# A hand-written order for the first three batches of an adaptive-norm state-space block on one core

## The reference, cut to what matters

```python
sa, ca, ga, sb, cb, gb = split(silu(c) @ wmod)          # per batch, 256 channels each; ga, gb kept away from 0
h = layernorm(x) * (1 + ca) + sa
u, gate = split(h @ W_in.T)                              # 256 and 256 channels
b, dt = u @ W_state.T, min(softplus(u @ W_dt.T + b_dt), 10)   # 128 states each
decay = exp(-dt * (softplus(A_log) + 1e-4))
state[t] = decay[t] * state[t-1] + (1 - decay[t]) * b[t]      # over the 512 tokens
x1 = x + ga * ((state @ W_C.T * silu(gate) + h * D) @ W_out.T)
h = layernorm(x1) * (1 + cb) + sb;  h_prev = h one token earlier
xk, xr = mix of h and h_prev by mu_k, by mu_r
out = x1 + gb * (sigmoid(xr @ W_r.T) * (relu(xk @ W_k.T)**2 @ W_v.T))
```

## Time and profile before

| what | value |
|---|---|
| median of 3 runs | 375.15 us |
| profiled execution | 375.2 us, its span 373.4 us |
| PE, DVE, ACT, POOL busy | 96%, 81%, 82%, 69% of the span |
| first matmul of step 3 (batch 0's K) | 47.80 us |
| first matmul of steps 4 and 5 | 68.39 and 89.63 us |
| last matmul starts, last DVE instruction ends | 367.2, 370.9 us |

### The profile page before, as it was taken

The page is one execution under the profiler, slowest core; times in us unless marked ns, Lnnn a source line. Parts: engine busy times, 40 slices in busy tenths (PEclk is TensorE's granted clock), DMA queues, the critical chain, the costliest instruction groups (busy, mean ns, idle before and its releaser), DMA issues.

```text
span 373.4 us, 5613 instructions
## 1 busy us (share of the span) xinstructions
PE 359.3 (96%) x1702; PEld 275.8 (74%) x1705; DVE 303.2 (81%) x640; ACT 307.7 (82%) x416; POOL 259.3 (69%) x269
## 2 busy tenths in 40 slices
PE   7999799999999999999999999999999999999784
PEld 4776477777778777777778777777877777776563
DVE  2788967988979798988979898888979788877654
ACT  4466779899898989989898989989898989977372
POOL 2072658969686887969686986968687894855560
PEclk9999999999999999999999999999999999999999
DMA  8931111130313132040313122040303021010111
GB/s 280 395 109 56 56 59 56 58 114 0 117 53 112 59 108 61 32 139 2 113 57 114 56 73 97 2 141 29 114 0 114 1 76 38 21 38 0 56 55 60
DMA packets 18607, 29.16 MB, mean 78 GB/s; under 512 B 1168, under 2 KB 9616, under 8 KB 18448
## 3 DMA queue, kind: packets, MB, share of 16 engines
q1 hardware_dynamic: 18144, 28.71, 22.6%
q10 hardware_dynamic: 432, 0.09, 0.1%
HBM read 20.40 MB, written 8.39 MB: 77 GB/s over the span
## 4 chain that ended last, share of the span: by engine, by line
POOL 46%; issue 39%; PE 7%; DVE 4%; ACT 2%; DMA 1%; POOLq 1%; SPq 0%; DVEq 0%; ACTq 0%
POOL xr_lo L773 10%; POOL xk_lo L773 7%; POOL z_lo L830 6%; POOL h_lo L773 6%; POOL k_lo L773 6%; POOL state_lo L820 4%; POOL rstd L783 3%; PE slot L224 3%; DMA w_in<-weights_in 1%; PE slot L238 1%; PE slot L352 1%; DVE stats L566 1%; POOL prev L814 1%; POOL spread L781 1%; POOL spread L780 1%
## 5 line engine op out<-in xcount | busy, mean ns | idle before, releaser
L809 POOL TENSOR_TENSOR rstd<-mv,half_neg 128x4 f32<-128x4 f32 x16 | 16.1, 1007 | 54.0 <-DVE mv L579 54.0
L452 ACT ACTIVATE prev<-slot,mod,mix_prev 128x512 f32<-128x512 f32 x64 | 46.3, 787 | 5.8 <-PE slot L231 5.8
L773 POOL TENSOR_TENSOR xk_lo<-xk,xk_hi 128x512 fp32r<-128x512 f32 x32 | 40.9, 1298 | 9.8 <-ACT xk_hi L463 9.0
L224 PE MATMUL slot<-h_hi,wf_hi 128*128 128x512 f32 x128 | 45.9, 399 | 0.4 <-ACT h_hi L478 0.4
L224 PE MATMUL slot<-h_hi,wf_lo 128*128 128x512 f32 x128 | 45.6, 397 | 0.0
L773 POOL TENSOR_TENSOR xr_lo<-xr,xr_hi 128x512 fp32r<-128x512 f32 x32 | 42.5, 1330 | 0.0
L830 POOL TENSOR_TENSOR z_lo<-z,z_hi 128x512 fp32r<-128x512 f32 x26 | 33.7, 1295 | 10.9 <-ACT z_hi L459 7.4
L773 POOL TENSOR_TENSOR k_lo<-k_act,k_hi 128x512 fp32r<-128x512 f32 x30 | 38.2, 1293 | 3.8 <-ACT k_act L533 3.8
L773 POOL TENSOR_TENSOR h_lo<-h,h_hi 128x512 fp32r<-128x512 f32 x30 | 38.4, 1303 | 3.1 <-ACT h_hi L478 3.1
L231 PE MATMUL slot<-ident,xn 128*128 128x128 f32 x256 | 35.9, 274 | 2.8 <-DVE xn L603 2.1
L231 PEld LDWEIGHTS slot<-ident,xn 128*128 128x128 f32 x256 | 29.7, 141 | 11.3 <-issue 4.7
(11 more groups left out here) (123 smaller groups left out, 1002.5 us busy)
## 6 DMA issues: line engine op xcount, KB each, us to landing
x_tok<-x_tok_in SPq DMA_DIRECT2D x16, 512.0 KB, 3.6
x_ch<-x_ch_in SPq DMA_DIRECT2D x16, 512.0 KB, 3.7
x_out<-wmod SPq DMA_DIRECT2D x15, 512.0 KB, 3.0
wmod<-wmod_in SPq DMA_DIRECT2D x1, 1024.0 KB, 10.1
w_in<-weights_in SPq DMA_DIRECT2D x1, 1024.0 KB, 11.5
w_in<-weights_in SPq DMA_DIRECT2D x1, 768.0 KB, 5.6
wmod<-wmod_in SPq DMA_DIRECT2D x1, 512.0 KB, 6.6
x_out<-wmod SPq DMA_DIRECT2D x2, 256.0 KB, 2.0
```

Of the source, the lines that this page charges most:

```text
L224: ins = nc.tensor.matmul(out, w[:, c, at + d * P:at + (d + 1) * P], x[:, c, :], start=first, stop=last)
L452: return nc.scalar.activation(prev[:, mix, i, 1:T + 1], ps_n[:, i, :], ACT.Identity, bias=mod_at(SHIFT2 + i, k), scale=mix_prev[:, mix, i, ...
L773: nc.gpsimd.tensor_tensor(lo, x, hi.bitcast(F32), ALU.subtract).then_inc(done, 1)
L809: nc.gpsimd.tensor_tensor(rstd2[:, c % 2], mv2[:, c % 2, 1, :], half_neg[:], ALU.pow).then_inc(rstd2_ok, 1)
```

## The change

The steps 0 to 2 are written out by hand and the loop starts at step 3. The order in each engine's list is new for these three batches. Loads: the early weights come in two transfers, first the 512 columns for L256 (512 KB), and the gate's 256 columns (256 KB) behind the first part of `wmod`; the rest of `wmod` now comes ahead of the third batch of tokens. Batch 0's front is not split: its `dt`, `b` and `g` are plain float32 products of `w_front`, `w_early` and `h`; with it `h_hi` and `h_lo` of batch 0 are gone. The front of batch 2 is emitted ahead of step 3. In PSUM, V and the `x1` transposes move to slot 3, K, the `xn2` transposes and (from batch 3 on) `g` to slot 2; `g` of batches 0 to 2 stays in slot 3 and the `x1` transposes of batch 0 in slot 2; the transposes of batches 1 and 2 for `h` go to slot 1. The `keep_warm` matmuls go from 13 + 11 + 5 + 6 to 10 + 4. In the loop one thing changes on PE: R's low piece of half 0 goes ahead of all of `y`. On ACT the halves of `h` are made in the order 0, 1 (before: 1, 0). `low_h(2)` stands on POOL, `h_lo` of batch 1 on DVE.

```diff
-        STEPS = range(0, NB + 4)
+        STEPS = range(3, NB + 4)
+        def ps_h(k):
+            return slot[1] if 0 < k <= WHOLE else slot[0]
+        def ps_gate(k):
+            return slot[3] if k <= WHOLE else slot[2]
+        def ps_x1(k):
+            return (slot[2] if k == 0 else slot[3])[:].rearrange(...)
...
 # SP
-            sp.dma_start(w_in[:, 0:CH * 3 * C], w_d[:, 0:CH * 3 * C]).then_inc(s_w, 16)
+            sp.dma_start(w_early[:, :, 0:GATE], w_early_d[:, :, 0:GATE]).then_inc(s_w, 16)
             sp.dma_start(wmod[:, :, 0:2 * C], wmod_cols[:, :, 0:2 * C]).then_inc(s_wmod, 16)
+            sp.dma_start(w_early[:, :, GATE:], w_early_d[:, :, GATE:]).then_inc(s_wgate, 16)
...
 # PE
-            keep_warm(slot[0][:, 0, :], 13)
+            keep_warm(slot[0][:, 0, :], 10)
...
+            first_norm(0)
+            keep_warm(slot[3][:, 0, :], 4)
+            pe.wait_ge(front_ok, 1)
+            pe.wait_ge(h0_ok, 1)
+            half(dt_out, w_front, 0, h[:, 0], 0, first=True)
+            pe.wait_ge(h_ok, 1)
+            half(dt_out, w_front, 0, h[:, 0], 1, last=True).then_inc(dt_ps, 1)
+            half(b_out, w_front, NS, h[:, 0], 0, first=True)
+            half(b_out, w_front, NS, h[:, 0], 1, last=True).then_inc(b_ps, 1)
+            pe.wait_ge(s_wgate, 16)
+            half(g_out, w_early, GATE, h[:, 0], 0, first=True)
+            half(g_out, w_early, GATE, h[:, 0], 1, last=True).then_inc(g_ps, 1)
+            modulation(4, 3, slot[2][:, 1, :])
+            state_out(0)
+            first_norm(1)
+            modulation(7, 5, slot[2][:, 1, 3 * NB:]).then_inc(mod_ps, 1)
+            attention_out(0, 0)
+            front_high(1)                 # dt and b, 8 matmuls; waits wsplit_lo, hhi_ok, z_ok[1]
+            front_low(1)                  # 4 matmuls
+            attention_out(0, 1)
+            gate_high(1); gate_low(1)     # 8 and 4 matmuls
+            first_norm(2)                 # waits x1_ok of batch 0
+            token_stats(0)                # the x1 transposes
+            state_out(1)
+            gate_high(2)                  # waits hhi_ok 2, silu_ok 2
+            front_high(2)                 # waits z_ok of batch 1
+            to_channels(ps_n, xn2).then_inc(t3_ps, 1)   # waits xn2a_ok, xn2b_ok
+            front_low(2); gate_low(2)     # wait hlo_ok
+            attention_out(1, 0); attention_out(1, 1)
...
 # PE, in the loop
+                if live(d):
+                    pe.wait_ge(xrlo_ok[0], d + 1)
+                    half(r_out, wl_hi, MIX_R, xr_lo, 0)
                 if live(b):
                     # y, high part (or state_out)
...
-                if live(d):
-                    pe.wait_ge(xrlo_ok[0], d + 1)
-                    half(r_out, wl_hi, MIX_R, xr_lo, 0)
...
 # ACT, ahead of the loop, in this order
+            ln1_apply(0); modulated(0, 0) -> h0_ok; modulated(0, 1) -> h_ok
+            exponential(0); decays(0); table load; ln1_apply(1); gate_silu(0)
+            wl_hi for K, R; modulated(1, 0..1); rounded_h(1); ln1_apply(2)
+            table load; exponential(1); decays(1); table load
+            wl_hi for V, OUT; wy_hi; gate_silu(1); modulated(2, 0..1); rounded_h(2)
+            table load; ln1_apply(3); previous x2 of batch 0; exponential(2)
+            previous x2; rounded_xk(0, 0); decays(2); rounded_xk(0, 1); table load; gate_silu(2)
 # DVE, ahead of the loop, behind the splitting of the early weights
+            ln1_stats(1); clipped(0); ln1_mean_variance(1); driven(0); scanned(0)
+            ln1_apply(1); ln1_stats(2); ln1_mean_variance(2); gated(0); ln1_apply(2)
+            h_lo of batch 1; rest_of_modulation(); clipped(1); ln1_stats(3); after_attention(0)
+            driven(1); scanned(1); ln1_mean_variance(3); after_transpose(0); gated(1)
+            normalised(0); ln1_stats(4); ln1_mean_variance(4); ln1_apply(3)
+            mixing(0, 0); clipped(2); mixing(0, 1); after_attention(1)
+            driven(2); scanned(2); after_transpose(1)
 # POOL, ahead of the loop
+            ln1_scale(0); ln1_scale(1); low part of K; ln1_scale(2); low parts of R, V
+            second_scale(0); ln1_scale(3); low_h(2); low parts of OUT and wy
```

More of the change, by code:

```diff
@@ new lines, in state_out, with attention_out @@
+            def state_out(k):
+                pe.wait_ge(state_ok, k + 1)
+                for i in range(CH):
+                    last = nc.tensor.matmul(ps_y[:, i, :], w_y[:, i * P:(i + 1) * P], state[:], start=True, stop=True)
+                last.then_inc(y_ps, 1)
+            def attention_out(k, i):
+                pe.wait_ge(h_ok, k + 2)
+                pe.wait_ge(z_ok[i], k + 1)
+                last = half(o_out, w_late, OUT, z, i, first=(i == 0), last=(i == CH - 1))
+                if i == CH - 1:
+                    last.then_inc(o_ps, 1)
@@ L449, in gate, with ln1_apply @@
                 nc.scalar.activation(r_gate[:], ps_r[:], ACT.Tanh, scale=0.5).then_inc(tanh_ok, 1)
+            def ln1_apply(k):
+                act.wait_ge(shift1_ok, k + 1)
+                before(act, t1_ps, k)
+                for t in range(TT // 2):
+                    last = nc.scalar.activation(xn1[:, t, :], x_tok[:, k % 3, t, :], ACT.Identity,
+                                                bias=shift1[:, k % 2, t:t + 1], scale=rstd1[:, k % 2, t:t + 1])
+                last.then_inc(xn1a_ok, 1)
             def previous(mix, i, k):
@@ new lines, in gate_silu @@
+            def gate_silu(k):
+                act.wait_ge(g_ps, k + 1)
+                before(act, yg_ok, k)
+                nc.scalar.activation(silu[:], ps_gate(k)[:], ACT.Silu).then_inc(silu_ok, 1)
+            ln1_apply(0)
+            act.wait_ge(mod1_ok, 1)
+            act.wait_ge(t1_ps, 1)
+            modulated(0, 0).then_inc(h0_ok, 1)
+            modulated(0, 1).then_inc(h_ok, 1)
+            exponential(0)
+            decays(0)
+            nc.scalar.preload_act_table_set("silu_and_others")
@@ L639, in _, with mixing @@
+            def mixing(k, i):
+                if i == 0:
+                    dve.wait_ge(first_ok, k + 1)
+                dve.wait_ge(prev_ok[i], k + 1)
+                for x, mix, done, low in ((xk, KEY, xk_ok, xklo_ok), (xr, REC, xr_ok, xrlo_ok))[::1 if i == 0 or k == LAST else -1]:
+                    before(dve, low[i], k)
+                    mixed(x, mix, i, k, done[i])
             nc.vector.memset(half_neg[:], -0.5).then_inc(consts_ok, 1)
@@ new lines, in _ @@
+            ln1_mean_variance(2)
+            gated(0)
+            ln1_apply(2)
+            for i in range(CH):
+                dve.wait_ge(hhi_ok, 1)
+                nc.vector.tensor_tensor(h_lo[:, i], h[:, 1, i], h_hi[:, i].bitcast(F32), ALU.subtract).then_inc(hlo_ok[i], 1)
+            rest_of_modulation()
+            clipped(1)
+            ln1_stats(3)
+            after_attention(0)
+            driven(1)
+            scanned(1)
+            ln1_mean_variance(3)
+            after_transpose(0)
@@ L669, in _ @@
+            gated(1)
+            normalised(0)
+            ln1_stats(4)
+            ln1_mean_variance(4)
+            ln1_apply(3)
+            mixing(0, 0)
+            clipped(2)
+            mixing(0, 1)
+            after_attention(1)
+            driven(2)
+            scanned(2)
+            after_transpose(1)
             for s in STEPS:
                 a, b, c, d = s, s - 1, s - 2, s - 3
+                if live(b) and b > WHOLE:
+                    scanned(b)
+                if live(c):
+                    normalised(c)
```

460 lines of the change are left out of this document (263 added, 197 removed).

## The result

The changed kernel takes 373.42 us, the median of seven runs (372.59 to 374.37), against 375.15 for the kernel before in the same series. It is 1.7 us faster in the median, where 3.3 were forecast. The ratio of the two sets of runs, which is not quite the quotient of the medians (0.9954), is 0.9943, with an interval of 0.9928 to 0.9958, so about 2.1 us. The profiled executions stand further apart, 375.2 and 372.59; the latter is the fastest of its seven. So the traces show 2.6 us, and 0.9 of the forecast's error lies between the runs and not in that trace.

The account below looks back on a forecast made before the run. PE, busy in 96% of the span, was taken as the bound; -2.3, +1.2, -2.4 and +0.1 up to step 4 made -3.3, loop and tail 0: 375.2 to 371.9 us, own range 370.5 to 373.3, stated range 370.0 to 374.1.

Parts of the forecast that it names:

- the walk: New engine order followed with trace prices to step 4's first matmul: 65.05 against 68.39; then loop and tail.
- Step A: Opening: less weight load ahead and only half 0 of h needed start batch 0's front at 11.95, not 14.24: -2.3 us.
- Step B: Batch 0's front on PE: 8 whole matmuls, 6.85 us, instead of 24 split ones, 5.6: +1.2 us.
- Step C: Opening behind 14.24: eleven zero matmuls gone, -2.4 us if the waits they stood in don't come back.
- D: Waits in the new order up to step 4: 3.05 us in sum against 2.95 before, +0.1; could be off by -1.5 to +2.
- one sign of being wrong: Opening: a PE wait over 1.5 us was listed among what would show the forecast wrong.
- rival 2: Opening's waits are longer: DVE's after_transpose pass comes once more into PE's path, 2.1 us, giving 374.0; chance 14%.
- Step E: Loop, 13 split steps: R's low piece ahead of y moves the wait to state_lo; 0, bounds -2.2 to +2.3 us.
- rival 1: Loop: state_lo is early enough, so R's piece ahead of y gains 0.17 us a step, giving 369.7; chance 8%.
- rival 4: Loop: the wait moved from state_hi to state_lo costs more, +2.3 us, giving 374.2; chance 3%.
- Step F: Tail: y of the last batch comes 0.47 later, but DVE's later wait absorbs it; 0, at worst +0.47 us.
- The clock: Opening: with 10 zeros PE runs at 1.2 GHz from 6.2 until batch 0's front, +4.4 us, giving 376.3; chance 5%.

Follow-up runs that it names:

- run 3: Changed kernel with R's low piece back behind y's high part in every step; 373.03 us, ratio to the kernel before 0.9942.
- run 5: Changed kernel with the early input weights in one transfer of 768 KB again; 373.94 us, ratio to the kernel before 0.9949.
- run 6: Changed kernel with batch 0's front split again and eleven zero matmuls instead of four; 374.58 us, ratio to the kernel before 0.9968.
- run 7: Changed kernel with batch 1's h transposes in slot 0 again; 381.15 us, ratio to the kernel before 1.0152.
- run 1: The changed kernel again, no edit; 373.26 us, 372.57 to 375.76 in ten runs, ratio to the kernel before 0.9952.
- run 9: Changed kernel with 8 and 5 zero matmuls in two PE waits of the tail; 372.95 us, ratio to the kernel before 0.9931.
- run 8: The kernel before with batch 0's front as whole products and nothing else of the change; 376.09 us, ratio to the kernel before 1.0003.
- run 4: Changed kernel with batch 2's state_hi ahead of the relu of K(0) in step 3; 372.31 us, ratio to the kernel before 0.9932.
- run 2: Changed kernel with 13 instead of 10 zero matmuls in front; 373.30 us, ratio to the kernel before 0.9942.
- run 10: Changed kernel with 12 instead of 10 zero matmuls in front and 2 ahead of the first modulation; 374.02 us, ratio to the kernel before 0.9955.
- run 11: Changed kernel with early state_hi of batch 2, zeros in the tail's waits and more zeros in the opening; 372.34 us, ratio to the kernel before 0.9916.
- run 12: The kernel before with 8 and 5 zero matmuls in the tail's waits; 374.94 us, ratio to the kernel before 0.9984.

## Why the prediction was right, and where its size was off

- **Which way, and where.** Right: the time is won between the start and step 4 (2.32 us in the traces), the loop gives 0.28 us, where the forecast had 0, and the tail nothing. The order of the waits in the opening and three of their sizes are as walked. The size was not: the median, 373.42, is 0.12 above the forecast's own range of 370.5 to 373.3 and lies in the stated one, to 374.1, only by the room that was left for the rivals, not by the walk; the gain is about half of what was forecast. Runs 3, 5, 6 and 7 each take one part of the change back; the new order on DVE and POOL, the zeros left out and batch 2's front ahead of step 3 were not tested singly, and what they give is read from the walk and the traces.
- **Step A** was 0.2 us too large in the trace (front at 12.12, not 11.95), 0.6 in run 1's. The term that failed is the landing of the first modulation's weights, which the walk took to be over when the weight product ends; from there to the modulation 0.2 us pass in the changed kernel's trace (8.22) and 0.7 in run 1's (8.60). In run 9's there is no such wait (7.88), and the front starts at 11.70, before the walk's time. The walk's other bound, `xn1` until 9.85, wasn't the last: it is ready at 9.84 and at 9.52 in these traces, and the transposes follow the modulation (10.03, 10.41). Part of the gain hangs on when loads land.
- **Step B** was right: the whole front took 6.95 us (12.12 to 19.07), 6.85 forecast. Run 6 shows that in the new order the unsplit front wins 0.6 to 0.9 us; run 8 that alone it wins nothing.
- **Step C** with **D**: step 3's first matmul was 0.13 late against the walk. Up to step 4 another 0.9 is lost. 0.67 of it is the wait for `xn2(1)`, 1.52 instead of 0.85: the walk had the wait but not that a DVE instruction stands still for POOL's subtraction (run 4 gets 0.64 back by one edit). The other 0.2 is spread over gaps, the largest 0.3 us ahead of the `h` transposes at 62.37. By the letter one sign of being wrong came up, a wait over 1.5 us on PE in the opening. It is rival 2 in kind, in a third of its size (0.67 of 2.1) and at another wait, `xn2(1)` and not `z(1)`.
- **Step E** was right in mechanism and size: 0.02 us a step between before and after, 0.00 between run 3 and the changed kernel. Rivals 1 and 4 are out.
- **Step F** was right: 50.51 us on both sides.
- **The clock** was weighed as one case, 5% for a loss large enough to turn the sign, and not as a loss in part of the runs. It was that: in the opening 1.6 us in run 3's profiled execution and about 1.7 in run 7's. In the changed kernel's own trace the rise came later than the walk had it: all ten zeros ran at the lower level and ended at 5.75, not 5.4. Of the seventeen runs of the changed kernel three are over 374.2 (374.37, 374.72, 375.76), but in the first two the span is 371.5 and 371.9, and 2.8 to 2.9 us lie outside it, 1 us more than in most runs; only the third, with a span of 373.6 and a clock of 0.990, looks like run 3's (373.4, 0.990). What came ahead of such a loss was ten zeros, of which at most three at the higher level, and waits of 0.4 to 0.9 us on one side or both of L334. That the fewer zeros are its cause isn't shown: in the 21 runs with more of them (2, 10 and 11) the longest span is 1.6 us over the shortest of its kernel, but run 9 has no such loss in six either.
- **The account.** By the traces: forecast -3.3; the wait for `xn2(1)` +0.7, the front's start +0.2, the loop -0.3, the rest +0.1 make -2.6. This pair of traces flatters the change: the span after, 370.8, is among the shortest, that before, 373.4, the longest of the ten runs beside run 1 with a granted clock of 0.996 or more (372.9 to 373.4). The changed kernel's four such runs there have 370.7 to 371.1, so 2.2 us less in the middle. With the tail filled on both sides it is 2.0 us (runs 9 and 12). All of these lie within the interval of the comparison, 1.6 to 2.7 us, as the median's 1.7 does. How much the landing of the load and how much the clock take of the difference to the trace is open, since most of the runs have no trace.

The Trainium skill says that the activity window of the clock gate runs freely, so that the same kernel warms up at another point in each run (TensorE: Matmul & The Clock Gate, section "What's actually happening"). The traces agree: PE changed pace at about 4.5 us in run 3, during the zeros; between the last zero's start (about 5.1) and L334 (6.16) in the changed kernel; and only at about 10 in run 7.

## What to carry to other kernels

A walk over the four lists with prices from the trace gave step 4 within 1.0 us. Two things that it lacked make 0.8 of that: when loads land one behind another, and which DVE instructions must stand still for POOL. A semaphore wait that is one of two nearly equal ones isn't removed by moving work past it; look first when the other operand is ready. And a wait on PE of two microseconds may cost half its length again (0.9 to 1.2 us behind 2.12), one of 2.86 cost 4.95: fill it with matmuls on zeros, as runs 9 and 12 do, and what you measure becomes steadier too. Read the gain from more than one trace: two single ones gave 2.6 us here, where the medians with a quiet tail give 2.0.

## What the runs showed of the hardware that I had not expected

- A wait of 2.1 us on PE was followed by about 3 us with the clock at 0.50 in six of eleven profiled executions that had it unfilled (runs 2, 3, 5, 7, 8, 10), at 0.9 to 1.2 us each where the rest of the tail could be compared. None of the three that had it filled (runs 9, 11 and 12) shows it. A wait of 2.86 in run 7 was followed by ten microseconds at 0.50.
- In run 3 waits of 0.88 and 0.48 us, with little work before and between, were followed by some 3 us at the lower level.
- A DVE subtraction of 128x4 numbers took 0.39 and 1.03 us instead of 0.17 when it met POOL's subtraction of 128x512, and ended with it both times.
- The granted clock in the windows reads 1.00 until the level has changed for the first time: so from 6 to 10 us in run 7, where L334 took twice its time. A late rise in the opening shows in the spacing of the matmuls and not in that figure.
